# Two convs on one Trainium2 core: tiles of two widths side by side in the second conv's rounds

## The reference

```
x = x + L0(group_norm(x))      # 3x3 conv, its 9 shifts and a 5x5 conv, folded into one 5x5 conv
x = x + L1(group_norm(x))      # quadratic 3x3 conv:
    spot = [1, the 9 pixels of the 3x3 window]             # 10 values
    out[o] = sum over c, i, j of filters[o, c, i, j] * spot[c, i] * spot[c, j]
```

## Time and profile before

| | |
|---|---|
| median of 3 executions | 304.87 us (304.46 to 305.16) |
| the profiled execution | 305.6 us |
| its span, first to last instruction | 303.9 us |
| TensorE busy (matmul) | 276.0 us, 91% |
| VectorE busy | 251.5 us, 83% |
| ScalarE busy | 88.1 us, 29% |
| GpSimd busy | 33.0 us, 11% |
| mean granted TensorE clock | 0.979 of full |

### The profile page before, as it was taken

One profiled execution on the slowest core, in us unless ns is written; L12 is line 12 of the kernel. 1 busy time (PEld: TensorE's weight loads), 2 busy tenths in 40 slices (PEclk: granted clock), 3 DMA queues, 4 the chain that ended last, 5 costly groups with the idle time before them and its releaser, 6 DMA issues.

```text
span 303.9 us, 13566 instructions
## 1 busy us (share of the span) xinstructions
PE 276.0 (91%) x6464; PEld 125.6 (41%) x6464; DVE 251.5 (83%) x216; ACT 88.1 (29%) x135; POOL 33.0 (11%) x82
## 2 busy tenths in 40 slices
PE   0579999899999999999999999999999999999930
PEld 0124443343334434436457455333334446447310
DVE  1899899995999999599999999976999999950330
ACT  5432016949258989529000000004000000000000
POOL 7913970000110000000000000000000000000000
PEclk9999999979999999999999999999999999999985
DMA  6973000000000000000000000085000000000049
GB/s 191 382 193 82 4 3 2 2 5 2 2 2 4 4 2 2 4 2 5 2 2 4 4 2 4 2 172 111 2 2 4 2 2 4 2 4 4 2 86 190
DMA packets 19206, 11.45 MB, mean 38 GB/s; under 512 B 17744, under 2 KB 17872, under 8 KB 19024
## 3 DMA queue, kind: packets, MB, share of 16 engines
q1 hardware_dynamic: 14640, 9.06, 11.7%
q10 hardware_dynamic: 4512, 1.53, 2.2%
HBM read 6.40 MB, written 4.19 MB: 35 GB/s over the span
## 4 chain that ended last, share of the span: by engine, by line
PE 80%; DVE 7%; ACT 3%; issue 3%; DMA 2%; SPq 1%; DVEq 0%
PE acc L1007 63%; PE acc L1050 15%; ACT raw L507 3%; DMA raw<-in_x 2%; DVE stats L741 2%; PE acc L1101 2%; DVE plane L759 1%; DVE raw L801 1%; DVE arena L669 1%; ACT arena L497 1%; DVE scaled L637 0%; DVE norm L756 0%; SPq L314 0%; SPq L321 0%; DVE mean_var L746 0%
## 5 line engine op out<-in xcount | busy, mean ns | idle before, releaser
L1007 PE MATMUL acc<-product,weight 32*32 32x512 f32 (+1 forms) x3040 | 128.6, 605 | 0.0
L1007 PEld LDWEIGHTS acc<-product,weight 32*32 32x32 f32 (+1 forms) x3040 | 61.7, 110 | 63.8 <-issue 51.1
L879 DVE TENSOR_TENSOR product<-plane 128x4096 f32<-128x4096 f32 x19 | 83.3, 4427 | 0.1
L1007 PE MATMUL acc<-raw,weight 32*32 32x512 f32 (+1 forms) x992 | 44.3, 605 | 0.0
L1050 PE MATMUL acc<-product,middle 32*64 32x512 f32 (+1 forms) x576 | 30.6, 621 | 0.0
L1007 PEld LDWEIGHTS acc<-raw,weight 32*32 32x32 f32 (+1 forms) x992 | 20.4, 111 | 20.7 <-issue 16.2
L801 DVE TENSOR_TENSOR raw<-acc,arena 128x512 f32<-128x512 f32 x16 | 9.9, 684 | 18.9 <-issue 18.7
L741 DVE BATCH_NORM_STATS2 stats<-raw 128x6 f32<-128x512 f32 x32 | 19.7, 686 | 3.1 <-DMA raw<-in_x 3.1
L879 DVE TENSOR_TENSOR raw<-plane 128x4096 f32<-128x4096 f32 x5 | 22.2, 4433 | 0.0
L1007 PE MATMUL acc<-product,arena 32*32 32x512 f32 (+1 forms) x448 | 22.0, 606 | 0.0
L507 ACT ACTIVATE raw<-arena 32x512 f32<-32x512 f32 x32 | 21.9, 683 | 0.5
(11 more groups left out here) (121 smaller groups left out, 213.9 us busy)
## 6 DMA issues: line engine op xcount, KB each, us to landing
raw<-in_x SPq DMA_DIRECT2D x8, 512.0 KB, 8.5
out<-raw SPq DMA_DIRECT2D x24, 128.0 KB, 2.9
arena<-in_L_conv_filters SPq DMA_DIRECT2D x4, 400.0 KB, 6.9
out<-raw ACTq DMA_DIRECT2D x8, 128.0 KB, 4.6
arena<-in_L_conv_w ACTq DMA_DIRECT2D x4, 100.0 KB, 4.0
w_in<-in_L_conv_w ACTq DMA_DIRECT2D x2, 36.0 KB, 1.9
w_in<-in_L_conv_w SPq DMA_DIRECT2D x2, 36.0 KB, 2.1
b_in<-in_L_conv_b SPq DMA_DIRECT2D x2, 0.5 KB
```

Source lines behind the costliest of these rows:

```text
L879: nc.vector.tensor_tensor(both_halves(g, u), plane_halves(g), plane_halves(g, PRODUCTS[k][0] * PITCH + PRODUCTS[k][1]), ALU.mult)\
L1007: return nc.tensor.matmul(acc[32 * s:32 * (s + strips), j, r, :], weights[32 * r:32 * r + 32, t:t + strips, :] .rearrange("p t c -> p (t c ...
```

## The change

In the second conv, `column` no longer gets a form. For each column of taps it makes one list of forms for the upper half (strips 0 and 1) and one for the lower half (strips 2 and 3), and runs them together round by round; `cell` issues one pair or two singles of one half. `None` stands for the single. The order in the list depends on what the upper half did last (`single_last`), and the callers lose their order of forms. Within a round the images are the outer loop and the halves the inner one.

```diff
-                if pairs:
-                    for d in range(lo + 1, hi + 1):
-                        last = pair(d, start and d == lo + 1, stop and d == hi)
+            single_last = [True]
+
+            def column(j, pixels, ys, weights, start, stop):
+
+                joint = list(range(ys[0] + 1, ys[-1] + 1))
+                if single_last[0]:
+                    upper = [None] + joint
                 else:
-                    for s in range(STRIPS):
-                        for r in range(GROUP):
-                            d, t = (lo, 0) if s % 2 else (hi + 1, hi - lo)
-                            last = tile(r, s, 1, d, t, start, stop)
+                    upper = joint + [None]
+                if len(joint) == 2:
+                    lower = [joint[0], None, joint[1]]
+                else:
+                    lower = upper[::-1]
+                if joint:
+                    single_last[0] = upper[-1] is None
+                for n in range(len(upper)):
+                    for r in range(GROUP):
+                        for s, d in ((0, upper[n]), (2, lower[n])):
+                            last = cell(j, pixels, ys, weights, r, s, d, start and n == 0,
+                                        stop and n == len(upper) - 1)
                 return last
```

In the second conv's opening, group 0's column off the even half now runs whole (3 rounds), then the first border batch, then the column off the odd half, then the second batch:

```diff
-                    for half in (0, 1):
-                        column(0, plane_pixels(0, half), every_row, sum_taps[0][:, 0:3, :], half == 0, False, PAIRS)
+                    column(0, plane_pixels(0, 0), every_row, sum_taps[0][:, 0:3, :], True, False)
                     edges0(1, ROW_SIDES)
-                    for half in (0, 1):
-                        column(0, plane_pixels(0, half), every_row, sum_taps[0][:, 0:3, :], False, False, SINGLES)
+                    column(0, plane_pixels(0, 1), every_row, sum_taps[0][:, 0:3, :], False, False)
                     edges0(1, COLUMN_SIDES)
```

In the first conv the pair rounds of "total" are split around the second border batch, the single round moves behind them, and the second part of group 1 begins with singles:

```diff
             edges0(0, ROW_SIDES)
-            product0(1, "total", 0, False, False, False)
+            product0(1, "total", 0, False, False, True, (-1, 0))
             edges0(0, COLUMN_SIDES)
-            product0(1, "total", 0, False, True, True).then_inc(part_done, 1)
+            product0(1, "total", 0, False, False, True, (1, 2))
+            product0(1, "total", 0, False, True, False).then_inc(part_done, 1)
             pe.wait_ge(edges_copied, 2)
-            rest0(1, PAIRS_FIRST)
+            rest0(1, SINGLES_FIRST)
```

```diff
+        def store_last(eng, strips, parity, done):
+
+            for r in range(GROUP):
+                eng.wait_ge(evicted, 3 * GROUP + r + 1)
+                store(eng, 1, r, strips + ((3,) if r % 2 == parity else ()), done)
...
+            store_last(sp, (0,), 1, stored)
...
+            store_last(pool, (2,), None, stored_by_pool)
...
-            for r in range(GROUP):
-                act.wait_ge(evicted, 3 * GROUP + r + 1)
-                store(act, 1, r, (2, 3))
+            store_last(act, (1,), 0, stored)
```

More of the change, by code:

```diff
@@ L302, in made, with store @@
             return len(MADE[0]) * g + MADE[g].index(stream) + 1
-        def store(eng, g, r, strips):
+        def store(eng, g, r, strips, done):
             for s in strips:
@@ L1000, in _, with cell @@
         def _(pe):
-            def column(j, pixels, ys, weights, start, stop, pairs):
+            def cell(j, pixels, ys, weights, r, s, d, first_one, last_one):
                 lo, hi = ys[0], ys[-1]
-                def tile(r, s, strips, d, t, first_one, last_one):
-                    return nc.tensor.matmul(acc[32 * s:32 * (s + strips), j, r, :],
-                                            weights[32 * r:32 * r + 32, t:t + strips, :]
+                if d is not None:
+                    return nc.tensor.matmul(acc[32 * s:32 * s + 64, j, r, :],
+                                            weights[32 * r:32 * r + 32, d - 1 - lo:d + 1 - lo, :]
@@ L1042, in plane_pixels, with column0 @@
                 return pixels
-            def column0(odd, stack, at, pitch, x0, every, five, start, stop, pairs):
+            def column0(odd, stack, at, pitch, x0, every, five, start, stop, pairs, rows):
                 def tile(r, s, strips, d, t, first_one, last_one):
@@ L1054, in column0 @@
                 if pairs:
-                    for d in range(-1, 3):
+                    for d in rows:
                         for s in (0, 2):
@@ L1064, in column0, with product0 @@
                 return last
-            def product0(g, name, odd, start, stop, pairs):
+            def product0(g, name, odd, start, stop, pairs, rows=range(-1, 3)):
                 if name == "next":
@@ L1070, in product0 @@
                     return column0(odd, plane[g], PLANE_AT - 2 * PITCH, PITCH, 2, 2, weight0[:, PAIR_AT:EDGE_AT, :],
-                                   start, stop, pairs)
+                                   start, stop, pairs, rows)
                 source, x0 = ("step", 1) if name == "step after" else (name, 0)
@@ L1077, in product0 @@
                 pe.wait_ge(middle_ready, g + 1)
-                return column0(odd, *half_at(g, source), x0, 1, five, start, stop, pairs)
+                return column0(odd, *half_at(g, source), x0, 1, five, start, stop, pairs, rows)
             def part(g, names, odd, forms):
@@ L1169, in mixed_unit, with side_unit @@
                     taps = (cross_taps if j else sum_taps)[0][:, 3:6, :]
[L1170 to L1175, removed]
+                return column(j, stream_pixels(g, UNIT_OF[name][0], j), every_row, taps, start, stop)
+            def side_unit(g, j, name, start=False):
                 pe.wait_ge(stream_made, made(g, name + (" right" if j else " left")))
@@ L1181, in side_unit, with taps1 @@
                     a = {"linear": 0, "square": 9}[name] + 6 * j
[L1182 to L1187, removed]
+                return column(j, stream_pixels(g, UNIT_OF[name][1], j), every_row, weight1[:, a:a + 3, :], start, False)
+            def taps1(g, j, u, stop=False):
                 k = 1 if u == NEXT else u - 5
@@ L1194, in taps1 @@
                     last = column(j, stream_pixels(g, u, half, shift), ys,
-                                  weight1[:, at:at + len(ys), :], False, stop and n == len(where) - 1, pairs)
+                                  weight1[:, at:at + len(ys), :], False, stop and n == len(where) - 1)
                 return last
@@ L1248, in _ @@
-                in_pairs = g == 0
+                    taps1(g, 1, NEXT).then_inc(unit_used, 1)
                 for u in range(7, LAST_UNIT):
                     wait_made(g, u)
[L1251 to L1259, removed]
+                    taps1(g, 0, u)
```

64 lines of the change are left out of this document (29 added, 35 removed).

## The result

The changed kernel takes 1951.88 us (median of 4 runs, 1943.68 to 1956.88) against 304.85 us: 6.40 times as long, with an interval of 6.38 to 6.43. The profiled execution took 1950.46 us around a span of 1948.7 us. The forecast was 298.8.

A forecast was written before the change was run, and what follows sets the result against it. TensorE alone was taken to bound images 4 to 7, and waits among TensorE, ScalarE and VectorE the part before 196 us. Terms -3.5 - 0.6 - 2.0 = -6.1 us gave a median of 298.8 us, range 288 to 312.

The forecast's parts named there:

- A: The forecast itself, chance 0.55: width changes cost 0 to 0.165 us, mixed rounds 0.875 to 0.93; 291 to 305 us.
- D: Rival, chance 0.16: two widths can't share the array; 964 one-width stretches in the second conv, about 1,080 us.
- changes of width: Second conv: 110 boundaries between rounds where halves change width, against some 42 before, each taken at 0.165 us.
- mixed round: Second conv: a round of 4 tiles of 64 and 8 of 32, 12 program matmuls, taken at 0.875 us.
- B: Rival, chance 0.12: changes between mixed rounds cost nothing; -15.0 us, 290 us.
- C: Rival, chance 0.12: the single half sets the mixed round's length; 326 us at 1.09 us a round, 312 at 0.98.
- The price of a single round: Second conv: 16 matmuls of 32x32 take 1.09 us, because something that grows with the number of matmuls binds.
- The borders: First conv: the 1.54 us stall and low clock (1.7) go, three more width changes cost 0.5; sum -2.7 us.
- The stores: Last 16 stores split over three engines: 0, hidden behind full DMA engines; upper bound +2 if GpSimd issues slower than 1 us each.
- Images 0 to 3: Second conv's first images: VectorE's chain and TensorE both reach the 176.94 us point 3.5 us earlier, then -0.6 us more.
- 4 to 7: Second conv's later images, where TensorE alone decides: 93.5 us against 95.5, so -2.0 us.

The follow-up runs named there:

- Experiments 1 to 3: The changed kernel with halves outside and images inside (376.66 us), with images two at a time (630.11 us), and in its own order all 32 wide (311.26 us).
- experiment 7: The kernel before with the two inner loops of a single round exchanged, so it goes image by image over the strips: 305.53 us, ratio 1.003.
- experiment 5: The kernel before with the first conv's new border order alone: 304.79 us, ratio 0.999.
- experiment 4: The changed kernel with the old second conv, leaving borders and stores: 305.84 us, ratio 1.003; also the kernel before with only the new second conv: 1951.13 us.

## Why the prediction was wrong

**The step that failed is the choice between A and D in "changes of width" (0.165 us, at a boundary between rounds).** The prediction took the local reading of the earlier trace rows: a width waits only for what its own position still works on. The rows of before could not tell it from the reading of rival D, since every position changed width at once; it said so, and gave the local one 0.55 against 0.16. The changed kernel's rows at 92.32 and 93.42 decide it: both loads go to idle strips and wait. Experiments 1 to 3 show it by their times: 196, 452 and 964 stretches, and with one width no waits. That the emptying itself is cheap was right (0.165 forecast; 1.00 less two passes of 0.43 leaves 0.14 in the mixed rounds at full clock). What is lost isn't the emptying, but the sharing: a change cuts off the overlap with all other positions. A mixed round was priced at 0.875 us, and is eight stretches of 1.00, one after another.

The rule that was cited, the Trainium skill, "TensorEngine Tiling (Array Packing)", Key Properties, that a change of the tiling mode and not just of the tile drains TensorE, holds here: each change between 32x64 and 32x32 tiles waits until the array has emptied, and a stretch of a pair or of two singles takes 1.00 and 1.01 us. The count in rival D was exact too, 964.

**Rival D's own size was also off**, 1,080 against 1,952. The term that was mis-sized is the 0.95 us a stretch, taken at full clock; 885 of the stretches ran at the lower level at 1.85 to 1.90. At full clock it was 1.00 to 1.01, which is some 60 us of the difference over 964 stretches. The kernel of two images a stretch, with the count of D and the clock at full, took 1155. So of the 1,647 us lost, some 850 are the alternations and some 800 the clock. The second number is a comparison of two kernels that differ in what a stretch holds, no exact split; the changed kernel's trace gives nearly the same, as 885 stretches that are each 0.84 to 0.89 us longer make some 770 us. That the clock could fall was not in any part of the prediction: ahead of its fall the array went from all 16 positions at work to two.

**Rivals B and C** never came into play; both need widths that share the array. The price of a single round, 1.09, was right (experiment 7), and so was its explanation in kind, as the all-32-wide kernel has pair rounds of 16 matmuls at 1.04 instead of 0.875.

**The borders, -2.7, were mis-sized: nothing to be measured came** (experiment 5: -0.25 us between medians, interval -0.9 to +0.3). In the changed kernel's trace the step looks right, as foretold. Its chain of waits from 59 to 67 us answers to the earlier trace rows:

```profile
59.72 1.90 PE acc L1066 x32
61.62 0.34 PE acc L1117 x5
61.96 0.19 issue
62.15 1.42 PE acc L1117 x75
63.57 3.79 PE acc L1066 x72
67.38 1.88 ACT arena L504
```

The 1.54 us stall is 0.19 us, and the clock, 0.66 in the earlier trace rows, is 1.00. But three of the experiments kept the old border order, and each was profiled once. Here is the kernel with the stores alone, its chain and its clock:

```profile
60.60 1.13 issue
61.73 1.42 PE acc L1106 x75
63.15 3.70 PE acc L1055 x64
66.88 1.88 ACT arena L504
...
60.00:66.00 6.00, 4.87 (x152) 2.67 (x143) 5.86 (x9) 4.95 (x15) 0.00 (x0) 1.00 0.02 4
```

The stall is there, the low clock is not: 64 pair records take 3.70 us where the earlier trace rows have 5.40. In the other two (mixed rounds alone, singles image by image) the stall is 0.81 and 1.27 and the clock 1.00 as well. So the low clock comes with the old order in only one of four profiles, and its 1.7 us couldn't be booked as if each execution lost them. The mean clocks of the timed executions say how often it may come. Of 57 with the old order (39 of the kernel before, 6 of the stores alone, 12 of singles image by image) 8 have a mean clock of 0.976 to 0.979 and take 306.2 to 307.8 us, and the others are at 0.981 or more; of the 23 of experiments 4 and 5, with the new order, none is under 0.982. So the new order may prevent a dip that comes in one execution of seven, worth some 0.3 us in the mean (2 us in 8 of 57), but 23 executions are too few to show it, and no trace shows where in the 8 the clock was low. What the order does remove is most of the stall: it is 0.8 to 1.5 us in the four profiles with the old order and 0.2 to 0.5 in the six with the new one whose chain passes there. Less three changes of width at 0.165 that is -0.2 to 0.8 us, too little for these runs. ScalarE's copy that hangs on it starts at 66.39, 66.88 and 67.46 in the three kernels with the old order, and at 66.57 with the new one alone; the second conv starts between 90.15 and 91.41 in the four profiles with the old order, and between 90.01 and 91.57 in the eight with the new one.

**The stores, 0, cost 2.0 us** (307.08 less 305.04 in that comparison). Their upper bound was right, its reason not: GpSimd issues at 0.7 us a store, under the 1 us that was named as the limit. What the DMA engines moved was less.

**Images 0 to 3 (-3.5, -0.6) and 4 to 7 (-2.0)** were sums over mixed rounds, the first with the -2.7 of the borders in it, and none of them could be tested. That changed borders and stores together (experiment 4) end up near the kernel before, 1.0 us slower, fits the two alone, -0.25 and +2.0, within their intervals.

## What to carry to other kernels

When the rows allow two readings of a wait because everything happened at once in them, price the change under both, and weigh the loss as much as the chance. A range that ends at 312 while a rival with a chance of 0.16 says 1,080 is a reason for a probe of one stretch, not for a choice. In packed TensorE work, count stretches of one tile shape, each with its passes and 0.14 to 0.18 us, and fill every stretch with as many positions as there are before the shape changes. Before a stall or a low clock is booked as a gain, see whether a second execution shows it.

## What the runs showed of the hardware beyond that

- TensorE can be 99% busy and at its lower clock: with one pair or two singles a stretch the granted clock was 0.51 over 600 us (and 0.51 over 3,400 us with each twice), with two pairs or four singles 1.00 over 1,000 us at 98% busy.
- The time of a stretch hardly depends on what it holds side by side: two singles 1.01 us, four 1.02, eight 1.04; a whole round of 16 singles 1.12.
- A stall of about 1 us in the first conv's eight pair rounds near 27 us comes and goes. Those rounds take 8.30 us in the changed kernel and 7.13 before; the kernel of the stores alone has it, that of the borders alone has not, and neither touches these rounds. Eight of the twelve profiles have it. Its cause stays open, and since it moves all that follows it, single traces can't tell a gain of less than 1 us at the borders.
- The stores' loss of rate with GpSimd as third issuer (182 to 208 GB/s against 208 to 223) is measured, its cause is not: the queue of GpSimd with its other packets, or the other split of the strips over the queues, would both explain it. It was not tried apart.
